# Moving a convolution's and a weight preparation's steps about in a five-engine kernel of two feed-forward layers

## What is computed

```
def layer0(x):
    att = softmax(mlp(cond))                    # 32 x 8 mixture of 8 experts
    y = einsum('boi,bih->boh', att @ weight, x) + att @ bias_k[:, :, None]
    A, B = gate @ lora_A, gate @ lora_B         # one pair for each of 8 groups of 256 rows
    return x + y @ kernel + bias + (y @ A.T) @ B.T + (y @ As.T) @ Bs.T

def layer1(x):
    c = conv1d(x, taps9, groups=4) + (cond @ c_weight.T)[:, :, None] + fside
    x1, x2 = split(c @ w12.T + b12)
    return x + (silu(x1) * x2) @ w3.T + b3
```

## Time and profile before

| | us |
|---|---|
| median of 3 runs | 838.28 |
| the three runs | 838.28, 838.53, 830.34 |
| the profiled execution, its own time | 831.89 |
| its span, first to last instruction | 829.8 |
| mean granted TensorE clock, share of full speed | 0.985 |

### The profile page before, as it was taken

How to read it: one execution, slowest core, us unless ns; L and a number is a source line. 1 busy time by engine, 2 the same in 40 slices (tenths; PEclk the granted TensorE clock), 3 DMA queues, 4 the chain that set the end, 5 groups by cost and what they waited for, 6 DMA issues and landing times.

```text
span 829.8 us, 10413 instructions
## 1 busy us (share of the span) xinstructions
PE 786.4 (95%) x3889; PEld 659.2 (79%) x3889; DVE 532.7 (64%) x634; ACT 208.1 (25%) x251; POOL 88.3 (11%) x59
## 2 busy tenths in 40 slices
PE   5998889999999999789999999999999989999998
PEld 4867678888888999668888877877778868888886
DVE  4855775264443479987777759766665795565552
ACT  4431101010010032233333326332233641111110
POOL 4440532323222000000000000000000000000000
PEclk9999999999999999899999999999999999999999
DMA  8966845455455896244455232277754764444441
GB/s 277 238 180 188 216 109 132 122 119 135 111 143 127 199 279 194 70 126 127 126 159 145 76 127 77 64 200 206 203 163 177 271 236 152 153 152 152 167 161 76
DMA packets 88379, 131.45 MB, mean 158 GB/s; under 512 B 11208, under 2 KB 66936, under 8 KB 85656
## 3 DMA queue, kind: packets, MB, share of 16 engines
q1 hardware_dynamic: 85136, 129.90, 53.4%
q10 hardware_dynamic: 3064, 0.90, 0.7%
q0 software_dynamic: 144, 0.21, 0.1%
HBM read 78.20 MB, written 51.72 MB: 157 GB/s over the span
## 4 chain that ended last, share of the span: by engine, by line
PE 72%; DVE 10%; DMA 8%; SPq 5%; issue 3%; ACT 2%; DVEq 0%; ACTq 0%
PE ps L1561 30%; PE ps L1804 25%; PE ps L1862 16%; DMA w_raw<-in_L_ffn_w 2%; DVE cr L1279 1%; DVE cf L1271 1%; SPq L438 1%; DMA w_scratch<-w_d 1%; SPq L592 1%; DMA x<-x_scratch 1%; DVE w_s_lo L1252 1%; DMA lora_b_scratch<-lb_c_lo 1%; DMA h_f<-h_scratch 1%; SPq L355 1%; DMA res<-r_scratch 1%
## 5 line engine op out<-in xcount | busy, mean ns | idle before, releaser
L1804 PE MATMUL ps<-cr,w_s_hi 128*128 128x512 f32 x512 | 159.5, 393 | 5.1 <-ACT s L915 4.9
L1804 PE MATMUL ps<-cr,w_a_hi 128*128 128x512 f32 x384 | 122.2, 400 | 10.7 <-DVE s L1357 6.0
L1804 PEld LDWEIGHTS ps<-cr,w_s_hi 128*128 128x128 f32 x512 | 96.5, 189 | 27.2 <-issue 4.0
L1804 PE MATMUL ps<-cr,w_s_lo 128*128 128x512 f32 x256 | 100.2, 391 | 0.0
L1804 PEld LDWEIGHTS ps<-cr,w_a_hi 128*128 128x128 f32 x384 | 73.3, 192 | 28.4 <-DVE s L1357 8.1
L1561 PE MATMUL ps<-wk_hi,y_hi 128*128 128x512 f32 x256 | 80.5, 395 | 0.3 <-issue 0.3
L1561 PE MATMUL ps<-wk_lo,y_hi 128*128 128x512 f32 x256 | 79.0, 390 | 0.0
L1561 PE MATMUL ps<-wk_hi,y_lo 128*128 128x512 f32 x256 | 78.9, 389 | 0.0
L1127 DVE TENSOR_TENSOR x_t<-ps,x_t 128x1024 f32<-128x1024 f32 x16 | 19.6, 1222 | 92.3 <-PE ps L1561 92.3
L741 POOL TENSOR_TENSOR x_t<-x_in,f_bias 128x1024 f32<-128x1024 f32 x16 | 63.3, 3960 | 143.0 <-DMA x_scratch<-x_t 143.0
L1499 DVE TENSOR_TENSOR res<-ps,res 128x512 f32<-128x512 f32 x56 | 38.6, 689 | 59.0 <-PE ps L1862 58.3
(11 more groups left out here) (176 smaller groups left out, 1255.4 us busy)
## 6 DMA issues: line engine op xcount, KB each, us to landing
x_scratch<-x_t SPq DMA_DIRECT2D x128, 64.5 KB, 2.1
x<-x_scratch SPq DMA_DIRECT2D x32, 258.0 KB, 7.4
x_in<-in_x SPq DMA_DIRECT2D x16, 512.0 KB, 5.3
r_scratch<-r_t SPq DMA_DIRECT2D x16, 512.0 KB, 3.1
raw<-in_L_ffn_w SPq DMA_DIRECT2D x64, 128.0 KB, 4.7
h_scratch<-s SPq DMA_DIRECT2D x32, 256.0 KB, 2.4
h_f<-h_scratch SPq DMA_DIRECT2D x8, 1024.0 KB, 5.9
res<-r_scratch SPq DMA_DIRECT2D x16, 512.0 KB, 5.0
```

Of the source, the lines that this page charges most:

```text
L1804: last = pe.matmul(o, l, r, start=first and q == 0 and n == 0, stop=q == 3 and n == 2, skip_group_check=True)
```

## The change

First phase. `POOL_WK` is now (0,): the lo parts of blocks 1 and 2 go from POOL to DVE. DVE copies the taps' input earlier (before `mix_t`), PE turns the taps behind `y_tile(0)`, ACT takes them before `split_y(1)`. PE makes LoRA B before and after block 3's products, and DVE takes it before `wk_lo_part(6)`. SP issues b3's load behind `first_group_lb` instead of before; ACT issues b12's eight loads later. `b3_s`, one `lb_c_lo` and one `r_t` swap addresses.

Convolution. `load_w12(0)` goes into new tiles at 64 and 68 KB, before the last tiles of x1 are stored. `store_a(0)`, c's second bias and `load_w12(1)` take other places among the `load_x8`. `c_staged` is gone. DVE's list is interleaved anew. Gate unit 0 asks for image 29 before b21 (for all 32 before), and for all 32 before b22.

Gate stage. In units 0 to 6, 7 and 9 to 14 ACT's `part_copy` stand ahead of `silu`. A 17th slot at 199.75 KB holds half B's t1, `w_a_raw` and `h_f[0]` move to 24 KB, and `load_a` waits for less and is issued before `store_w3`. In units 9 to 14 DVE makes `a_lo` first and `w3_sums` later. Output stage: `add` 2 to 6 of unit 0 are set among the lo parts. The core of the diff:

```diff
-                for n, ks in (("hi", (162.25, 186.25)), ("lo", (199.75, 203.75)))]
+                for n, ks in (("hi", (162.25, 186.25)), ("lo", (90, 203.75)))]
-        raw2 = at("w_a_raw", [P, 2, PH, P], 199.75)
+        raw2 = at("w_a_raw", [P, 2, PH, P], 24)
+        raw_first = [at(f"raw_first{s}", [P, NL], 64 + 4 * s) for s in range(2)]
-        POOL_WK = (0, 1, 2)
+        POOL_WK = (0,)
-        LO_B, HI_B = dict(zip(PRODUCTS, (14, 1, 5, 3, 4, 12, 8))), ...
+        LO_B, HI_B = dict(zip(PRODUCTS, (14, 1, 5, 16, 4, 12, 8))), ...
@@ sync
-            wait_slot(sp, raw_of(5))
-            sp.dma_start(b3_s[:, :], b3.partition_broadcast(P)).then_inc(b3_in, 16)
...
             first_group_lb(sp, 0)
+            wait_slot(sp, raw_of(7))
+            sp.dma_start(b3_s[:, :], b3.partition_broadcast(P)).then_inc(b3_in, 16)
             sp.wait_ge(lora_taken, N_LORA)
...
+            sp.wait_ge(la_gathered, NG)
+            load_w12(0)
             store_x1(TILES - 4, 0, TILES - 1)
...
-            load_c_bias(1)
...
             load_x8(5)
-            for s in range(2):
-                sp.wait_ge(r_stored[s], 16 * TILES // 2)
-            load_w12(0)
-            for t in range(6, 12):
-                load_x8(t)
-            store_a(0)
+            for t in range(6, 9):
+                load_x8(t)
+            store_a(0)
+            load_x8(9)
+            load_c_bias(1)
+            for t in range(10, 12):
+                load_x8(t)
+            for s in range(2):
+                sp.wait_ge(r_stored[s], 16 * TILES // 2)
             load_w12(1)
...
-                    sp.wait_ge(w_lo_made, 4 * n)
+                    sp.wait_ge(w_lo_made, 4 * n - 2)
...
+                if 9 <= u <= 13:
+                    load_a(u)
                 if 9 <= u <= 12:
                     store_w3(u - 9)
-                if 9 <= u <= 13:
-                    load_a(u)
@@ scalar, gate_unit of units 1 to 6 (of 9 to 14: all of a_hi behind g_mm, then the copies)
                 part_copy(u, 0)
                 a_hi(n, 0)
                 a_hi(n, 1)
+                part_copy(u, 1)
                 silu(u, 0)
-                part_copy(u, 1)
                 s_hi(n, 0)
                 s_hi(n, 1)
                 part_copy(u, 2)
                 silu(u, 1)
@@ vector, the convolution: the new order
+            take_c(0), turn_w12(0, 0), take_c(1), take_c(2), turn_w12(0, 1), take_c(3), take_c(4),
+            weight_sums(0), take_c(5), take_c(6), s_lo(0, 0), take_c(7), s_lo(0, 1), take_c(8),
+            a_lo(0, 0), take_c(9), a_lo(0, 1), take_c(10), take_c(11), c_lo b11, take_c(12), take_c(13),
+            c_lo b21, take_c(14), take_c(15), c_sum t3, take_c(16), take_c(17), c_sum t1, take_c(18),
+            take_c(19), c_sum t2, take_c(20) to take_c(22), c_sum t4, take_c(23), take_c(24), c_lo t2,
+            take_c(25), take_c(26), c_lo t1, take_c(27), take_c(28), c_lo t3, take_c(29) to take_c(31),
+            c_lo b22, c_lo t4
...
             U7 = HALF_UNITS - 1
             hidden_a(U7 - 1)
-            dve.wait_ge(g_mm, 7 * U7 + 2)
             c_sum(LO_B["t1"], 15, 14)
...
                 hidden_a(u - 1)
                 weight_sums(n)
+                a_lo(n, 0)
+                a_lo(n, 1)
+                s_lo(n, 0)
+                part_add(u, 0)
+                s_lo(n, 1)
                 if k is not None:
                     turn_w3(k, 0)
+                    turn_w3(k, 1)
+                    w3_sums(k, 0)
+                part_add(u, 1)
...
             add(0, 0, 0, 32)
             w3_lo_part(4)
+            w3_lo_part(5)
             add(0, 0, 1)
-            w3_lo_part(5)
+            add(0, 0, 2)
             w3_lo_part(6)
+            add(0, 0, 3)
@@ tensor
             y_tile(0, 0, 16, True)
+            turn_taps()
             small_turns()
...
-            for k in range(3, 5):
-                dst, dst1 = first_u(0, k), first_u(1, k)
-            turn_taps()
             lb_result_mm(0)
             lb_result_mm(1)
-            dst, dst1 = first_u(0, 5), first_u(1, 5)
-            pe.wait_ge(taps_made, 1)
+            dst, dst1 = first_u(0, 3), first_u(1, 3)
+            pe.wait_ge(lora_taken, 4)
             lb_result_mm(2)
             lb_result_mm(3)
-            for k in range(6, 8):
+            for k in range(4, 8):
                 dst, dst1 = first_u(0, k), first_u(1, k)
```

More of the change, by code:

```diff
@@ L170, in layered_kernel @@
         s3 = at("s3", [P, HALF], 196.25)
-        r_t = [at(f"r_t{s}", [P, NL], 199.75 + 4 * s) for s in range(2)]
-        b3_s = at("b3_s", [P, NL], 90)
+        r_t = [at(f"r_t{s}", [P, NL], k) for s, k in enumerate((90, 203.75))]
+        b3_s = at("b3_s", [P, NL], 199.75)
         QH = KT // 2
@@ L627, in gate_unit @@
                     load_c(0, LO_B["b21"])
+                    load_a(HALF_UNITS)
                 if u == HALF_UNITS:
@@ L833, in _ @@
             la_hi_part(0)
+            act.wait_ge(taps_mm, 1)
+            for half in range(2):
+                last = act.activation(taps[:, :, half, :].rearrange("p g (q o) -> p g q o", q=PH),
+                                      bank(6 + half).rearrange("p (q g o) -> p g q o", q=PH, g=GRP), ACT.Copy)
+            last.then_inc(taps_made, 1)
             split_y(1, 0, 1)
@@ L844, in _ @@
                 act.dma_start(f_bias[:, :], f0_bias.partition_broadcast(P)).then_inc(fbias_in, 16)
-                for m in range(4):
-                    for h in range(2):
-                        act.dma_start(b12_s[32 * m:32 * m + 32, h, :],
-                                      b12.rearrange("(h m j b) -> h m b j", h=2, m=4, j=NJ)[h, m]).then_inc(b12_in, 16)
             wk_hi_part(6)
             wk_hi_part(7)
-            act.wait_ge(taps_mm, 1)
-            for half in range(2):
-                last = act.activation(taps[:, :, half, :].rearrange("p g (q o) -> p g q o", q=PH),
-                                      bank(6 + half).rearrange("p (q g o) -> p g q o", q=PH, g=GRP), ACT.Copy)
-            last.then_inc(taps_made, 1)
             for n in range(4):
@@ L860, in _ @@
             split_y(3, 1, 1)
+            with nc.allow_non_contiguous_dma(reason="a few columns of small arrays"):
+                for m in range(4):
+                    for h in range(2):
+                        act.dma_start(b12_s[32 * m:32 * m + 32, h, :],
+                                      b12.rearrange("(h m j b) -> h m b j", h=2, m=4, j=NJ)[h, m]).then_inc(b12_in, 16)
             for k in range(4, 6):
@@ L930, in gate_unit @@
                 n = prep_in(u)
+                if u > HALF_UNITS:
+                    act.wait_ge(g_mm, 7 * u)
+                    if n is not None:
+                        a_hi(n, 0)
+                        a_hi(n, 1)
+                    part_copy(u, 0)
+                    if n is not None:
+                        s_hi(n, 0)
+                        s_hi(n, 1)
+                    part_copy(u, 1)
+                    silu(u, 0)
+                    part_copy(u, 2)
+                    silu(u, 1)
+                    return
                 part_copy(u, 0)
-                if n is not None:
-                    a_hi(n, 0)
-                    a_hi(n, 1)
+                a_hi(n, 0)
+                a_hi(n, 1)
+                part_copy(u, 1)
                 silu(u, 0)
-                part_copy(u, 1)
-                if n is not None:
-                    s_hi(n, 0)
-                    s_hi(n, 1)
+                s_hi(n, 0)
+                s_hi(n, 1)
                 part_copy(u, 2)
@@ L950, in _ @@
             part_copy(U7, 0)
-            silu(U7, 0)
             act.wait_ge(g_mm, 7 * U7 + 2)
@@ L954, in _ @@
             part_copy(U7, 1)
+            silu(U7, 0)
+            part_copy(U7, 2)
             act.wait_ge(c_sum_made, 4 + 1)
-            act.wait_ge(g_mm, 7 * U7 + 4)
-            part_copy(U7, 2)
             c_hi_part(LO_B["t1"], HI_B["t1"])
@@ L1171, in _ @@
             wk_lo_part(5)
+            for n in range(4):
+                lb_lo_part(n)
             wk_lo_part(6)
             wk_lo_part(7)
-            for n in range(4):
-                lb_lo_part(n)
             take_z(0, 0, True)
@@ L1229, in turn_w12 @@
                 dve.transpose(dst.rearrange("p q (m b) -> p q m b", m=4),
-                              raw[half][:, :].rearrange("p (m a q) -> p q m a", m=4, q=PH)).then_inc(turned, 1)
+                              (raw if n else raw_first)[half][:, :].rearrange("p (m a q) -> p q m a", m=4, q=PH)).then_inc(turned, 1)
                 dve.wait_ge(turned, 2 * n + half + 1)
@@ L1306, in _ @@
             dve.wait_ge(c_bias_loaded[0], 16)
-            for b in range(8):
-                take_c(b)
+            take_c(0)
             turn_w12(0, 0)
+            take_c(1)
+            take_c(2)
+            turn_w12(0, 1)
+            take_c(3)
+            take_c(4)
+            weight_sums(0)
+            take_c(5)
+            take_c(6)
+            s_lo(0, 0)
+            take_c(7)
```

(12 more changed lines are left out.)

84 lines of the change are left out of this document (44 added, 40 removed).

## The result

The changed kernel takes 801.66 us (median of 4 executions, 800.24 to 803.84) against 836.95 us for the kernel before beside it (median of 4, 830.34 to 838.53). The ratio is 0.9617, 95% interval 0.958 to 0.9654: faster by 3.8%. (The quotient of the two medians is 0.958.) I had forecast 811 us in a range of 803 to 823. By the profiled executions the span fell from 829.8 to 798.4 us, 31.4 us, where my sum had 24.5.

The account below looks back on a forecast made before the run. PE, busy 786.4 of 829.8 us, was taken as the bound, with its late waits and half clock. 2.3 + 8.5 + 2.1 + 6.9 + 4.7 = 24.5 us gave 807.4 profiled, 813.8 as median; forecast 811, range 803 to 823.

Parts of the forecast that it names:

- the five places: Where PE's waits fall: first phase, convolution with gate unit 0, unit 7, units 9 to 12, output head; 29.9 us together.
- signs of "right": Trace signs to confirm the forecast, from the first phase to the output head, including two or three slow-clock stretches, not six.
- First phase, 2.3 forecast: Start to the convolution: earlier LoRA B lets PE resume 1.2 us earlier, and 1.5 of clock less 0.4 goes; 2.3 us.
- I give that load 1.2 us: First phase: SP's load of group 1's LoRA B comes 1.2 us earlier; bounds -1.5 and +4.
- The head: Program head: moving DVE's copy of the taps' input before mix_t gives zero, at most 0.9 us if held by POOL.
- Convolution and unit 0, 8.5 forecast: Early w12 and DVE's new order bring t3's start from 360.9 to 351.4; 8.5 us taken, bounds 2 and 12.
- A wait of 4 us stays, for DVE's two turns: Unit 0: PE reaches t3 at about 347.5 and still waits 4 us, until 351.4.
- Rival D: Convolution: each us store_a(0) lands after 300.8 costs the program one; landing at 330 gives 843 us; chance 0.02.
- Unit 7, 2.1: Unit 7: slot 16 and ACT copying before silu remove waits of 0.7 and 1.4; 2.1 us, bounds 0 and 2.1.
- Units 9 to 12, 6.9: Units 9 to 12: waits of 4.6 and 0.6 and clock loss of 1.7 go; 6.9 us, bounds 2 and 6.9.
- Rival C: Units 9 to 12 keep their waits because w3's loop of store, landing, load and turn sets the pace; 818 us; chance 0.08.
- Output head, 4.7: Output head: add 2 comes earlier; the 3.1 wait and 1.7 of clock go, less 0.1; 4.7 us, bounds 1.5 and 4.8.

Follow-up runs that it names:

- experiment 10: The changed kernel with DVE's two lo parts of the a weights moved from behind images 8 and 9 to behind image 14; 801.38 us (ratio 0.9607).
- experiment 6: The changed kernel with b12's eight loads early again on ScalarE's queue, ahead of the last two hi parts of wk; 800.87 us (ratio 0.963).
- experiment 5: The changed kernel with DVE's four lo parts of LoRA B behind the last two lo parts of wk again; 801.88 us (ratio 0.9597).
- experiment 4: The changed kernel with DVE again waiting for unit 7's second gate matmul group before its first block sum of t1; 801.77 us (ratio 0.9607).
- experiment 1: The changed kernel with DVE's order in the output head put back as before the change; 806.13 us (ratio 0.9658).
- experiment 3: The changed kernel with SyncE's order in units 9 to 12 put back, w3 stores ahead of the next a load; 809.32 us (ratio 0.9717).
- experiment 2: The changed kernel with DVE's order in units 9 to 14, and the counts the a loads wait for, put back; 829.12 us (ratio 0.9932).
- experiment 7: The changed kernel with y_bias and the next x tile issued on SyncE ahead of the slot wait and x tile 3; 803.06 us (ratio 0.9624).

## Why the prediction was right, and where its sizes were off

**What it said and what came.** The direction and the five places hold. Every size was too low, and three lie beyond the upper bound that I had set: unit 7 and units 9 to 12, whose bounds were the waits' own sums, and by 0.2 us the output's head. Of the signs of "right" these came: no PE wait for LoRA B near 64 us, PE's wait for a `part_copy` (at 345.7, said 348), no wait over 0.5 us in the gate units 7 to 15, none at the output's head, two stretches at half clock. DVE turns w12 at 277.92 (said 283) and takes the last image at 335.4 (said 341); the first image itself is 4.8 earlier. Two signs did not come: DVE's share from 282 to 302 is 14.04 of 20 us, 70% (said over 75), and PE's wait for group 1's LoRA B is 2.9 us (said about 5). Of "wrong" one sign came: DVE's wait for the store was 5.8 us, over the 5 that I had set, and it didn't matter (experiment 10).

**First phase, 2.3 forecast, 4.8 by the traces** (4.4 against the mean of the runs). My account was three late waits in a row, the last of them paid by DVE's list. The three waits are as I had them, but the account of the last is only half right. I let the half clock behind PE's return be covered by that wait, with DVE's list as it was. In the traces PE does come later to that place with half clock (17.8 to 19.2 us after its return, 16.6 without), but DVE's list is also shorter, by 1.6 us and more, because its second `y_lo` pair no longer runs beside GpSimd (1.30 us against 4.96 in the kernel before and 4.87 in experiment 6). This is the contrast of 4.47 and 1.29 in the earlier trace rows, which I had counted at the head of the program and not here. No run takes the two effects apart. From PE's return to the first image they gave 1.9 us (195.6 to 193.7) for my 1.1; the other 2.9 are PE's earlier return (83.55 against 86.44), for my 1.2.

"I give that load 1.2 us": SyncE issued it at 75.67, 3.5 us earlier than the earlier trace rows, since the issues of the eight stores before it took 9.4 us (59.59 to 69.03) where they had taken 13.5 (60.06 to 73.57); in the other runs it was issued at 75.0 to 77.1, in experiment 5 at 78.0. The wait near 64 is gone as said, and the 0.7 us for y lo is there; what I did not have is 1.9 us for `y_f` just before, where the kernel before has 1.0. What brought it is not LoRA B's order (experiment 5) nor b12's loads (6), each alone; what paces the landing of the stores of LoRA B, and so the load behind them, stays open.

**The head.** The copy that I moved ahead of `mix_t` took 0.40 us, beside a GpSimd operation of 2.35 us on the same stretch:

```profile
9.83 2.35 POOL L728 TENSOR_TENSOR wk_lo<-raw,wk_hi 128x1024 fp32r<-128x1024 f32 x1 [3.00 <-ACT wk_hi L811]
```

```profile
11.29 0.40 DVE L1097 COPY wpad<-w_raw 64x144 f32<-64x144 f32 x1 [0.51 <-DMA fside_s<-in_fside_S]
11.70 0.69 DVE L1100 COPY mix_t<-ps 128x512 f32<-128x512 f32 x1
```

No block until 12.2 us: zero, as in the sum. The Trainium skill (SBUF — State Buffer, "Who interferes with whom") says that such a copy can contend for the port pair shared with GpSimd and is then held until GpSimd is done; for this copy the trace shows no such hold.

**Convolution and unit 0, 8.5 forecast, 10.2 measured.** Bounded by 2 and 12. The last image was taken by 335.8, 5.1 us before my 340.9, of which 4.8 are the start; so the sum from there on is right within a us, and so is the start of t3 (345.71 and 4.8 against my 351.4). But its terms failed and cancelled. DVE was busy for 52.2 of the 58.5 us, one `c_lo` more included, where I had 54.3: consecutive instructions overlap by some 0.08 us (one ends at 311.93, the next began at 311.85), and fewer waits stand between them now. The small gaps were 0.5, not 2.0. The store held DVE for 5.8 instead of 2.6 us: it took 11.1 us to land (287.08 to 298.18), as in the earlier trace rows, where I had let it take 9.3 for 1.5 MB less ahead of it, and DVE was there at 292.5. "A wait of 4 us stays, for DVE's two turns" is the 3.38 us at 345.71, for the very copy behind the turns; the 1.8 for the third copy, which I laid over the clock loss, is not there. The half clock of 3.4 us took that time from it: PE arrived late. Where the half clock does not come, the third copy has 1.4 us of wait (experiments 4 and 6), so the cover that I had counted on is there.

**Rival D's premise fell.** "From 300.8 on each us that it lands later is a us of the program, since DVE has no slack": experiment 10 takes 5.8 us out of DVE's list and nothing moves, so those 5.8 us cost nothing. Behind them DVE is held to PE's images and to the landing of the image stores.

**Unit 7, 2.1 against 3.2** (with unit 8): the waits were 2.1, but the sum was made of waits alone (below). And the 4.69 us that DVE stood before `c_sum` t1 were not what PE paid: experiment 4 gives slot 16 0.5 us.

**Units 9 to 12, 6.9 against 8.5.** All five waits went and the clock loss of 1.7. What I missed is what a short wait costs beside its printed length: 8.5 - 5.2 - 1.7 = 1.6 us over five waits, 0.3 each. Experiment 1 has the same 0.3 beside its 3.1, and experiment 3, at the full clock, 0.9 beside three waits of 5.9 in units 10 to 12. Rival C, w3's loop as the pace, isn't true of the change. It is true of experiment 2; in experiment 3 the loop goes by the w3 stores and the a load behind them, and DVE waits for the a weights (18.1 us in four waits), not for w3.

**Output head, 4.7 against 5.0.** As said, in this pair of traces; 3.4 of it hold without the clock.

**The time.** 24.5 of the 31.4 us were seen; 2.5 of the miss are the first phase, 1.7 the convolution, 2.7 the waits' 0.3 us and unit 8. By the profiled execution's measure that is 800.24 for my 807.4, and by this measure even the 803.9 with the convolution at its upper bound is too high. I took the middle between that measure and the median's. Of the 6.4 us between the two 1.4 are left after the change: its four executions lie within 3.6 us. Why the kernel before spreads more stays open.

## What to carry to other kernels

Price a wait of PE that goes at its printed length and, in this kernel, 0.3 us more, and count the half clock behind it as a chance, not as a term. Where a two-input DVE operation and a GpSimd operation can meet, ask of every such pair whether they still meet after the change: here one pair cost 4.9 us or 1.3. Before you take one edit of a pair alone, close the ring: follow a load, its user, the step that frees its buffer and the queue in front of the next issue, and compare the round with the length of the unit; here 28.4 us against 19.04 made half of a good change 27 us worse than the whole. And an engine whose list ends last is not yet the bound: take its largest wait away, and look whether the waits behind it add up to the same, before you count on it.

## What the hardware showed that I had not expected

The half clock doesn't come behind every wait of the same length at the same place. At the output's head it came behind 3.1 us in the kernel before (682.6 us) and not behind 3.1 us in experiment 1. In unit 0 it came behind 3.4 us in the change and 3.1 in experiment 7, and not behind 3.35 us in experiment 4 nor 3.2 in experiment 6. In the kernel before it came behind 1.94 us at 565.1 and not behind 1.93 at 608.1, the same place two units later. Behind LoRA B's load it came for 2.9 us and more (3.4 or 6.8 us long) and neither for 2.6 us there nor for the 2.8 of the kernel before. Half clock can also cost nothing. In unit 0 the stretch to unit 1 is as long without it (experiment 4). Between 82.6 and 89.4 us it took 2.9 us of PE's time, and in all twelve traces that have it the wait of 3.2 us with its own half clock, which the two without it have, is gone.
